# A graph layer and a mixture layer on one core: seven tiles instead of eight in the mixture's last block

## The chip, the cores and the metric

The kernel runs on one core of a Trainium2 chip. The metric is the device time of one execution in microseconds (us): lower is better. A core has five engines with queues of their own: TensorE (PE in the profile, its weight loads PEld), VectorE (DVE), ScalarE (ACT), GpSimd (POOL) and SyncE (SP), which here only issues DMAs. They are held together by semaphores alone.

## What is computed

There are 10000 tokens of 512 channels. A graph layer (edge messages, two matmuls with batch normalisation over all tokens) is followed by a mixture layer. The change touches the mixture layer alone; `x` below is the input plus the graph layer's output.

```python
grouped = x.reshape(B, S // t, t, D)                 # groups of t = 16 tokens
cont_logits = einsum('bgtd,des->bgtes', grouped, controller) + tie
cont_perm = (cont_logits == max over the 16 tokens)  # 16 experts x 4 sets
intermediate = einsum('bgtd,desf->bgtesf', grouped, f1)
inner = relu(einsum('bgtesf,bgtes->bgesf', intermediate, cont_perm))
inter2 = einsum('bgesf,esfd->bgesd', inner, f2)
result = einsum('bgesd,bgtes->bgtd', inter2, cont_perm)
out = x + result                                     # input: layernorm(x)
```

Each group of 16 tokens is computed apart from the others, so tokens can be cut into tiles at any multiple of 16.

## The kernel before, in words

The graph layer runs first: the edges, then the up and down matmuls. It leaves its second activation, transposed, in the DRAM tensor `h2T`. Then `mixture` (L834) starts. It takes the tokens in **tiles** of 128 (`P`) and the tiles in **blocks** of 8 (`TB`), so a block is 1024 tokens (`BW`) and there are 10 blocks (`NB`, 10000 / 1024 rounded up): 80 tiles. 10000 tokens are 78.125 tiles. The ninth block ends at token 9216, and the last one is put so that it ends at token 10000: `row` (L901) has it begin at 10000 - 1024 = 8976. Its first 240 tokens are therefore computed twice, with the same result.

A tile has a **front** half and a **back** half. The front of tile j does: bring in 256 columns of `h2T` for two tiles (`load_h`, L1033), apply silu (`nonlinear`, L1265), turn it (`turn_g`, L1310) and add it to x (`new_tile`, L1165), store that sum in `x1d` (`store_x1`, L1047), normalise it (`stats`, `norm`), turn it again (`turn_x`, L1323), multiply by the controller (`logits`, L1332), find the maxima (`select`, L1189), turn the choice (`spread` on PE, `turn_p`, L1342), and sum the chosen tokens into `yT` (`sums`, L1347, copied by ACT in `to_yT`, L1272). When all tiles of a block have been through that, four `inner` steps (L1417) multiply the block's whole `yT` by `f1`; their relu (L1010) is shared by DVE and ACT and fills `inner_bd`. The back of tile j then does: spread the choice over rows (`rows`, L1374, and `back_rows`, L1213), four `unit` steps of matmuls with `f2` (`inter`, L1386, L1401 is their line), whose results ACT copies (L1293) and DVE takes the remainder of (L1226), eight matmuls of `final` (L1413, L1414), an add of x (`result`, L1229), and the store (`store_out`, L1059); x comes back from `x1d` by `load_back` (L1052).

The order of all this is written out by hand in one generator, `schedule(front, back)` (L924), which every engine walks and from which it picks its own steps. `blocks` (L912) calls it 11 times, unrolled: the front of block k goes with the back of block k - 1. In step m of the eight steps of a call, the engines do `sums` of front tile m, `logits` and `turn_x` of front tile m + 1, `turn_g` of front tile m + 2, and the whole back of tile m. `inner` 0 of the front block is at the end of the call, `inner` 1 to 3 are in step 0 of the next one. The 11th call has no front (`k` is None): it is a tail of eight steps of back alone. No step of the mixture is inside a hardware loop, and every wait is on a constant.

TensorE's part of one step with front and back is, in order: `turn_p` (L1345), `rows` (L1382), 32 matmuls of L1401, `turn_g` (L1319), `turn_x` (L1329), `sums` (L1367), `logits` (L1339), `final` (L1413, L1414). All of them are 32-bit, and those of L1401, L1433 and L1339 show in the trace as two matmuls each.

Of the kernel before, what the change touches and what calls it, by code (L numbers as in the profile page):

```python
# [9 lines left out]
ACT = mybir.ActivationFunctionType  # L10
AX = mybir.AxisListType

N, H = 10000, 512
# [20 lines left out]
TB = 8  # L34
BW = TB * P
NB = -(-N // BW)
F2P = 4
QB = ES // GT
GH = GB // 2
# [794 lines left out]
def mixture(nc, sem, psum, ident, mhalf, x, h2T, x1d, vec, controller, f1, f2, out, stats2):  # L834
# [3 lines left out]
    with ExitStack() as ctx:  # L838
# [62 lines left out]
        def row(k, j):  # L901


            if isinstance(k, int) and k * TB + j >= (NB - 1) * TB:
                return N - BW + (k - (NB - 1)) * BW + j * P
            return k * BW + j * P

        def by2(t, par, of):

            return (t - par) * (of // 2) + of  # L910
# [8 lines left out]

        def exists(k, j):  # L920

            return k is not None and not (isinstance(k, int) and k == NB - 1 and j >= TB)

        def schedule(front, back):  # L924

            if front is not None and static(front, 1):
                yield "silu", (0, 0, KH)  # L930
                yield "silu", (1, 0, KH)
                yield "turn_g", 0
                yield "stats", 0
                yield "norm", 0
                yield "turn_x", 0
                yield "logits", 0
                yield "turn_g", 1
                yield "stats", 1
                yield "select", 0
                yield "norm", 1  # L940
            for m in range(TB):
                new, next_ = exists(front, m + 2), exists(front, m + 1)
                u = m * QB
                if front is not None:
                    yield "spread", m
                if back is not None:
                    yield "rows", m
                if back is not None and m == 0:
                    yield "inner", 1
                    yield "unit", u  # L950
                    yield "low", u
                    if new:
                        yield "turn_g", m + 2
                    yield "inner", 2
                    yield "unit", u + 1
                    yield "low", u + 1
                    if new:
                        yield "stats", m + 2
                    if next_:
                        yield "turn_x", m + 1  # L960
                    yield "inner", 3
                    yield "unit", u + 2
                    yield "low", u + 2
                    if next_:
                        yield "logits", m + 1
                    yield "unit", u + 3
                    yield "low", u + 3
                    if front is not None:
                        yield "sums", m
                elif back is not None:  # L970
                    yield "unit", u
                    yield "low", u
                    yield "unit", u + 1
                    yield "low", u + 1
                    yield "unit", u + 2
                    yield "low", u + 2
                    yield "unit", u + 3
                    if new:
                        yield "turn_g", m + 2
                    yield "low", u + 3  # L980
                    if new:
                        yield "stats", m + 2
                    if next_:
                        yield "turn_x", m + 1
                    if front is not None:
                        yield "sums", m
                    if next_:
                        yield "logits", m + 1
                else:
                    if new:  # L990
                        yield "turn_g", m + 2
                        yield "stats", m + 2
                    if next_:
                        yield "turn_x", m + 1
                    yield "sums", m
                    if next_:
                        yield "logits", m + 1
                if next_:
                    yield "select", m + 1
                if new:  # L1000
                    yield "norm", m + 2
                if exists(front, m + 3 + (m + 1) % 2):
                    yield "silu", ((m + 4) // 2, (m % 2) * KH // 2, (m % 2 + 1) * KH // 2)
                if back is not None:
                    yield "final", m
                    yield "result", m
            if front is not None:
                yield "inner", 0
# [13 lines left out]
        with nc.Block() as block:  # L1022
            @block.sync
            def _(sp):
# [8 lines left out]
                def load_h(k, p):  # L1033
                    pair = k * (TB // 2) + p
                    if not static(pair, 2):
                        sp.wait_ge(t1, (pair - 1) * 2)
                    sp.dma_start(h2[p % 2][:, :, :], h2T[:, :, bass.ds(row(k, 2 * p), 2 * P)].rearrange("m p n -> p m n"))\
                        .then_inc(ldh[p % 2], 16)

                def load_x(k, j):  # L1040
# [49 lines left out]

                blocks(sp, body)
                for b in range(2):
                    sp.wait_ge(ots[b], 16 * (TB // 2) * NB)

            @block.gpsimd
            def _(pool):
# [37 lines left out]
                def body(k, kb):  # L1134
                    for what, n in schedule(k, kb):
                        if what == "spread" and kb is None:
                            keep(k, n)
                        if what == "rows" and k is not None:
                            keep(k, n)
                        if what == "stats":  # L1140
                            root(k, n)
                        if what == "norm":
                            split(k, n)
# [118 lines left out]
            def _(act):  # L1262
                act.wait_ge(nrm[5], 1)

                def nonlinear(k, p, c0, c1):  # L1265
                    pair = k * (TB // 2) + p
                    act.wait_ge(ldh[p % 2], by2(pair, p % 2, 16))
                    for c in range(c0, c1):
                        nc.scalar.activation(h2[p % 2][:, c, :], h2[p % 2][:, c, :], ACT.Silu, bias=sh[:, c:c + 1],
                                             scale=sc[:, c:c + 1]).then_inc(gr, 1)  # L1270

                def to_yT(k, j, c, r):  # L1272
# [36 lines left out]
            def _(pe):  # L1309
# [76 lines left out]
                def inter(k, kb, u):  # L1386
                    j, b, q = u // QB, u % QB, unit_of(kb, u)
                    if b < 2:

                        pe.wait_ge(yr, (k * TB + j if k is not None else NB * TB) * KH)  # L1390
                    if static(kb, 1) and u == 0:
                        pe.wait_ge(wf2, 16 * F2P)
                    if j == 0:

                        pe.wait_ge(inv, (kb * QB + b + 1) * 2)
                        pe.wait_ge(ina, (kb * QB + b + 1) * 2)
                    if not static(q, QB):
                        pe.wait_ge(ilr, q - QB + 1)
                    for i in range(NS):
                        e = QE * b + i  # L1400
                        last = nc.tensor.matmul(bI[b][32 * i:32 * i + 32, :],  # L1401
                                                ibd[:, e, j, :, :].rearrange("p s g -> p (s g)"), f2s[:, e, :],
                                                start=True, stop=True)
                    last.then_inc(ip, 1)

                def final(k, kb, j):
                    pe.wait_ge(rr, kb * TB + j + 1)
                    if not static(kb * TB + j, 1):
                        pe.wait_ge(otr, kb * TB + j)
                    pe.wait_ge(yr, (k * TB + j) * KH + 2 if k is not None else NB * TB * KH)  # L1410
                    for b in range(QB):
                        pe.wait_ge(ilr, unit_of(kb, j * QB + b) + 1)
                        nc.tensor.matmul(bF[:, :], rbd[:, b, :], ihi[b][:, :], start=(b == 0), stop=False)  # L1413
                        nc.tensor.matmul(bF[:, :], rbd[:, b, :], ilo[b][:, :], start=False, stop=(b == QB - 1))\  # L1414
                            .then_inc(fp, 1)

                def inner(k, q):  # L1417

                    if q == 0:
                        if static(k, 1):  # L1420
                            pe.wait_ge(wf1, 16 * KH)
                        pe.wait_ge(yr, (k + 1) * TB * KH)
                    else:
                        if q == 1 and not static(k, 1):
                            pe.wait_ge(otr, k * TB)
                        if q >= 2:
                            pe.wait_ge(inv, (k * QB + q - 1) * 2)
                            pe.wait_ge(ina, (k * QB + q - 1) * 2)
# [107 lines left out]
```

## Time and profile before

| | us |
|---|---|
| three runs | 2109.22, 2110.25, 2110.86 |
| median | 2110.25 |
| the profiled execution, its own time | 2105.35 |
| its span | 2103.6 |
| mean granted clock of TensorE in it | 0.972 of full |
| the mixture's share of the span | about the last 890 us |

The profiled execution is one more run, 4.9 us below the median of the three. Its span goes from its first instruction to the last DMA; 1.75 us of its own time lie around the span. All steps and rows in this document are in us from the start of that span. In the trace's rows, a matmul's length is modelled and neighbours overlap: the distance from one start to the next says what an instruction takes of the engine. An idle time in brackets behind a row says how long the engine had nothing to do before it, and what ended that; "issue" is an idle time for which the profile shows no one that was waited for. A row of busy time by windows gives the stretch, its length, then busy time and (instructions) of PE, PEld, DVE, ACT and POOL, and last TensorE's granted clock, the share of the DMA engines' time and GB/s. A row of waits gives who waited for whom: us in total, times, the longest.

### The profile page before, as it was taken

What the parts mean: (1) busy time and instruction counts of PE and PEld (TensorE: products, weight loads), DVE (VectorE), ACT (ScalarE), POOL (GpSimd) and SP (SyncE); (2) the same over time, 40 slices, a digit from 0 to 9 for tenths busy, and PEclk for the clock granted to TensorE, in tenths of its full rate; (3) what the DMA queues carried; (4) which work ended last, traced back from release to release, by engine and by line L of the source; (5) the groups of instructions that cost most, each with busy time, mean ns of one, the idle gap of its engine ahead of it and who ended that gap; (6) DMA issues with size and microseconds to landing.
All of it is one profiled execution on the core that took longest, in us unless ns stands there. A gap on an engine that the chain in (4) does not pass through costs nothing. (4 is left out here: it accounts for less than half of the span.)

```text
span 2103.6 us, 42031 instructions
## 1 busy us (share of the span) xinstructions
PE 1892.0 (90%) x15720; PEld 1362.7 (65%) x15720; DVE 1194.2 (57%) x2533; ACT 1003.9 (48%) x1742; POOL 386.7 (18%) x481
## 2 busy tenths in 40 slices
PE   0777389999999979999999678999999999999999
PEld 0233178888888858888888565665666666656564
DVE  1457266666566443333333356776766767667666
ACT  0354123333333265565656255565655656556553
POOL 1577230000000000000000141222222222222210
PEclk9998699999999989999999889999999999999999
DMA  9887655666566353343433283343433434334322
GB/s 378 213 156 130 121 154 158 192 181 170 156 190 183 116 183 129 138 154 118 174 117 136 79 288 110 122 131 117 137 117 108 145 108 145 107 117 137 113 75 76
DMA packets 182816, 309.18 MB, mean 147 GB/s; under 512 B 33065, under 2 KB 107305, under 8 KB 179594
## 3 DMA queue, kind: packets, MB, share of 16 engines
q1 hardware_dynamic: 169674, 285.35, 43.5%
q0 software_dynamic: 8960, 20.98, 5.2%
q8 instruction: 101, 1.65, 0.3%
q10 hardware_dynamic: 4032, 0.80, 0.2%
q14 instruction: 49, 0.40, 0.1%
HBM read 172.20 MB, written 134.87 MB: 146 GB/s over the span
## 5 line engine op out<-in xcount | busy, mean ns | idle before, releaser
L1401 PE MATMUL bank<-f2s,inner_bd 128*32 128x512 f32 x2560 | 299.0, 596 | 1.9 <-DVE inner_bd L1012 1.4
L1293 ACT ACTIVATE inter_hi<-bank 128x512 fp32r<-128x512 f32 x320 | 191.1, 597 | 223.1 <-PE bank L1401 221.0
L1226 DVE TENSOR_TENSOR inter_lo<-bank,inter_hi 128x512 fp32r<-128x512 f32 x320 | 220.9, 690 | 100.3 <-ACT inter_hi L1293 98.8
L608 ACT ACTIVATE h1o<-bank,b_by_channel 128x500 f32<-128x500 f32 x160 | 108.5, 678 | 326.7 <-PE bank L423 326.7
L421 PE MATMUL bank<-ahi,w_hi 128*128 128x500 f32 x640 | 250.7, 392 | 14.6 <-DVE alo L762 14.6
L421 PE MATMUL bank<-hhi,w_hi 128*128 128x500 f32 x640 | 251.3, 393 | 2.5 <-DVE hlo L569 2.5
L423 PE MATMUL bank<-hhi,w_lo 128*128 128x500 f32 x640 | 249.6, 390 | 0.0
L422 PE MATMUL bank<-alo,w_hi 128*128 128x500 f32 x640 | 249.2, 389 | 0.0
L422 PE MATMUL bank<-hlo,w_hi 128*128 128x500 f32 x640 | 249.0, 389 | 0.0
L423 PE MATMUL bank<-ahi,w_lo 128*128 128x500 f32 x640 | 248.8, 389 | 0.0
L575 DVE BATCH_NORM_STATS2 stats<-h1o 128x500 f32 (+1 forms) x160 | 103.6, 676 | 162.4 <-ACT h1o L608 162.4
L762 DVE TENSOR_TENSOR alo<-a_whole,ahi 128x500 fp32r<-128x500 f32 x160 | 108.8, 680 | 106.2 <-ACT ahi L798 106.2
L1275 ACT ACTIVATE yT<-bank 128x512 f32<-128x512 f32 x320 | 165.4, 604 | 6.8 <-PE bank L1367 1.1
L1401 PEld LDWEIGHTS bank<-f2s,inner_bd 128*32 128x32 f32 x2560 | 73.7, 109 | 136.2 <-issue 127.5
L768 DVE BATCH_NORM_STATS2 stats<-h2o 128x500 f32 (+1 forms) x80 | 52.6, 678 | 175.6 <-ACT h2o L806 175.6
L421 PEld LDWEIGHTS bank<-ahi,w_hi 128*128 128x128 f32 x640 | 120.6, 188 | 42.3 <-DVE alo L762 18.0
L1413 PE MATMUL bank<-inter_hi,back_bd 128*128 128x512 f32 x320 | 132.6, 414 | 9.4 <-ACT yT L1275 8.6
L421 PEld LDWEIGHTS bank<-hhi,w_hi 128*128 128x128 f32 x640 | 120.6, 189 | 26.7 <-DVE hlo L569 2.9
L423 PEld LDWEIGHTS bank<-ahi,w_lo 128*128 128x128 f32 x640 | 120.7, 189 | 25.1
L422 PEld LDWEIGHTS bank<-hlo,w_hi 128*128 128x128 f32 x640 | 120.8, 189 | 24.7
L423 PEld LDWEIGHTS bank<-hhi,w_lo 128*128 128x128 f32 x640 | 120.6, 188 | 24.8
L422 PEld LDWEIGHTS bank<-alo,w_hi 128*128 128x128 f32 x640 | 120.9, 189 | 23.9
(124 smaller groups left out, 3182.6 us busy)
## 6 DMA issues: line engine op xcount, KB each, us to landing
h1T<-h1o SPq DMA_DIRECT2D x19, 2000.0 KB, 8.1
h1in<-h1T SPq DMA_DIRECT2D x19, 2000.0 KB, 9.6
aggregate<-zeros SPq DMA_DIRECT2D x20, 1024.0 KB, 8.2
h2in<-h2T SPq DMA_DIRECT2D x40, 512.0 KB, 4.1
x<-in_x SPq DMA_DIRECT2D x80, 256.0 KB, 2.8
x<-x SPq DMA_DIRECT2D x80, 256.0 KB, 3.6
x_back<-x SPq DMA_DIRECT2D x80, 256.0 KB, 3.2
out<-x_back SPq DMA_DIRECT2D x80, 256.0 KB, 2.8
```

What stands on the lines that cost most here:

```text
L421: nc.tensor.matmul(out, w_hi[:, k, cols], a_hi[:, k, :], start=(k == 0), stop=False)
L422: nc.tensor.matmul(out, w_hi[:, k, cols], a_lo[:, k, :], start=False, stop=False)
L423: last = nc.tensor.matmul(out, w_lo[:, k, cols], a_hi[:, k, :], start=False, stop=(k == chunks - 1))
L575: nc.vector.bn_stats(stats1[:, m, bass.ds(c * 6, 6)], h1o[b][:, m, :]).then_inc(str_, 1)
L608: nc.scalar.activation(h1o[b][:, m, :], mb[m % 4][:, 0:CW], ACT.Identity, bias=b1c[:, m:m + 1]).then_inc(evr, 1)
L762: nc.vector.tensor_tensor(alo[b][:, k, :], aw[:, k, :], ahi[b][:, k, :].bitcast(F32), ALU.subtract).then_inc(lor, 1)
L768: nc.vector.bn_stats(stats2[:, m, bass.ds(c * 6, 6)], h2o[b][:, m, :]).then_inc(str_, 1)
L1226: nc.vector.tensor_tensor(ilo[u % QB][:, :], bI[u % QB][:, :], ihi[u % QB][:, :].bitcast(F32), ALU.subtract).then_inc(ilr, 1)
L1275: nc.scalar.activation(yT[:, c:c + 2, :, j * GB + r * GH:j * GB + (r + 1) * GH], bY[c // 2][r][:, :].rearrange("p (c e g) -> p c e g", c=2 ...
L1293: nc.scalar.activation(ihi[n % QB][:, :], bI[n % QB][:, :], ACT.Copy).then_inc(ihr, 1)
L1401: last = nc.tensor.matmul(bI[b][32 * i:32 * i + 32, :], ibd[:, e, j, :, :].rearrange("p s g -> p (s g)"), f2s[:, e, :], start=True, stop=True)
L1413: nc.tensor.matmul(bF[:, :], rbd[:, b, :], ihi[b][:, :], start=(b == 0), stop=False)
```

## The change

The number of tiles becomes a constant of its own, `NT` = 79 (10000 / 128 rounded up), and the last block has `TL` = 7 tiles, from token 10000 - 896 = 9104 on. A new helper `tiles(k)` gives the number of tiles of a block, and `exists` asks for it. `schedule` runs over the larger of the two counts: in the call with the front of the last block and the back of the ninth, step 7 has a back but no front, and the 11th call has seven steps. The last pair of the last block is one tile wide: its load of `h2T` and its silu have 128 columns in place of 256. `inner` and its relu keep the width of eight tiles, and the eighth place of `yT` keeps what the ninth block left there; nothing reads the result. Waits that were worked out from eight tiles are worked out from `NT`.

```diff
+NT = -(-N // P)
+TL = NT - (NB - 1) * TB
...
-            if isinstance(k, int) and k * TB + j >= (NB - 1) * TB:
-                return N - BW + (k - (NB - 1)) * BW + j * P
+            if k * TB + j >= (NB - 1) * TB:
+                j += (k - (NB - 1)) * TB
+                return N - TL * P + j * P
...
-            return k is not None and not (isinstance(k, int) and k == NB - 1 and j >= TB)
+            return k is not None and k * TB + j < NT
+        def tiles(k):
+            return 0 if k is None else TL if k == NB - 1 else TB
...
-            for m in range(TB):
+            for m in range(max(tiles(front), tiles(back))):
+                ahead, behind = m < tiles(front), m < tiles(back)
-                if front is not None:
+                if ahead:
                     yield "spread", m
-                if back is not None:
+                if behind:
                     yield "rows", m
-                if back is not None and m == 0:
+                if behind and m == 0:
...
-                    if front is not None:
+                    if ahead:
                         yield "sums", m
-                elif back is not None:
+                elif behind:
...
-                if back is not None:
+                if behind:
                     yield "final", m
                     yield "result", m
...
+                    width = min(2, tiles(k) - 2 * p) * P if p < TB // 2 else 2 * P
-                    sp.dma_start(h2[p % 2][:, :, :], h2T[:, :, bass.ds(row(k, 2 * p), 2 * P)]...
+                    sp.dma_start(h2[p % 2][:, :, 0:width], h2T[:, :, bass.ds(row(k, 2 * p), width)]...
...
-                    sp.wait_ge(ots[b], 16 * (TB // 2) * NB)
+                    sp.wait_ge(ots[b], 16 * ((NT + 1 - b) // 2))
...
-                        if what == "rows" and k is not None:
+                        if what == "rows" and n < tiles(k):
                             keep(k, n)
...
-                        nc.scalar.activation(h2[p % 2][:, c, :], h2[p % 2][:, c, :], ACT.Silu, ...
+                        nc.scalar.activation(h2[p % 2][:, c, 0:width], h2[p % 2][:, c, 0:width], ACT.Silu, ...
...
-                        pe.wait_ge(yr, (k * TB + j if k is not None else NB * TB) * KH)
+                        pe.wait_ge(yr, (k * TB + j if k is not None else NT) * KH)
...
-                    pe.wait_ge(yr, (k * TB + j) * KH + 2 if k is not None else NB * TB * KH)
+                    pe.wait_ge(yr, min((k * TB + j) * KH + 2, NT * KH) if k is not None else NT * KH)
...
-                        pe.wait_ge(yr, (k + 1) * TB * KH)
+                        pe.wait_ge(yr, (k * TB + tiles(k)) * KH)
```

## Rows read from the trace of the kernel before

**Rows 1.** The page: busy time of each engine, share of the span, instructions.

```profile
PE 1892.0 (90%) x15720; PEld 1362.7 (65%) x15720; DVE 1194.2 (57%) x2533; ACT 1003.9 (48%) x1742; POOL 386.7 (18%) x481
```

**Rows 2.** Busy time by windows: steps 5, 6, 7, transition, tail.

```profile
2013.12:2022.36 9.24, 9.24 (x78) 5.89 (x77) 7.25 (x15) 5.05 (x9) 2.68 (x5) 1.00 0.26 85
2022.36:2031.14 8.78, 8.78 (x74) 5.45 (x73) 5.26 (x10) 5.01 (x9) 1.95 (x3) 1.00 0.21 63
2031.14:2039.42 8.28, 7.38 (x62) 3.90 (x60) 4.39 (x7) 4.46 (x8) 0.29 (x1) 1.00 0.22 65
2039.42:2057.25 17.83, 15.32 (x557) 10.77 (x557) 7.49 (x14) 5.39 (x12) 0.00 (x0) 1.00 0.10 32
2057.25:2100.39 43.14, 43.14 (x309) 19.99 (x307) 28.39 (x42) 16.73 (x28) 0.00 (x0) 1.00 0.27 86
```

**Rows 3.** Timeline of PE, from step 4's end in the tenth call to the end.

```profile
2012.88 0.40 PE L1414 MATMUL bank<-inter_lo,back_bd 128*128 128x512 f32 x1
...
2017.29 0.66 PE L1319 MATMUL bank<-ident,h2in 128*128 128x128 f32 x4
2017.79 0.60 PE L1329 MATMUL bank<-ident,xn 128*128 128x128 f32 x4
...
2020.43 0.47 PE L1413 MATMUL bank<-inter_hi,back_bd 128*128 128x512 f32 x1
...
2022.13 0.40 PE L1414 MATMUL bank<-inter_lo,back_bd 128*128 128x512 f32 x1
...
2030.91 0.40 PE L1414 MATMUL bank<-inter_lo,back_bd 128*128 128x512 f32 x1
...
2037.43 0.47 PE L1413 MATMUL bank<-inter_hi,back_bd 128*128 128x512 f32 x1 [0.90 <-ACT yT L1275]
...
2039.11 0.39 PE L1414 MATMUL bank<-inter_lo,back_bd 128*128 128x512 f32 x1
...
2093.86 0.39 PE L1414 MATMUL bank<-inter_lo,back_bd 128*128 128x512 f32 x1
...
2100.00 0.39 PE L1414 MATMUL bank<-inter_lo,back_bd 128*128 128x512 f32 x1
```

**Rows 4.** SP's and DVE's timelines: a load of x, its add, and the last add.

```profile
2083.16 2.08 SPq L1057 DMA_DIRECT2D x_back<-x  x1
```

```profile
2088.14 0.69 DVE L1233 TENSOR_TENSOR x_back<-bank,x_back 128x512 f32<-128x512 f32 x1 [0.82 <-PE bank L1414]
...
2100.43 0.69 DVE L1233 TENSOR_TENSOR x_back<-bank,x_back 128x512 f32<-128x512 f32 x1 [0.82 <-PE bank L1414]
```

**Rows 5.** DMA issues of the mixture: KB each, median us to landing.

```profile
x_back<-x SPq DMA_DIRECT2D x77, 256.0 KB, 3.2
...
h2in<-h2T SPq DMA_DIRECT2D x32, 512.0 KB, 4.1
```

**Rows 6.** SP's and ACT's timelines: last load of h2T, first silu on it.

```profile
1980.93 0.38 SPq L1037 DMA_DIRECT2D h2in<-h2T  x1
```

```profile
1993.30 1.11 ACT L1269 ACTIVATE h2in<-h2in,shift,scale 128x256 f32<-128x256 f32 x2
```

**Rows 7.** PE's waits in two transitions, 2039.4 to 2057.2 and 1955.9 to 1974.2.

```profile
PE bank L1433 <- issue: 2.0, 2, 1.2
PE bank L1401 <- issue: 0.4, 1, 0.4
```

```profile
PE bank L1433 <- issue: 2.8, 3, 1.6
```

**Rows 8.** Windows of 1200 to 1300; PE's timeline at the mixture's start.

```profile
1200.00:1300.00 100.00, 71.28 (x987) 53.02 (x987) 57.15 (x154) 50.59 (x98) 37.49 (x54) 0.85 0.60 205
```

```profile
1217.81 0.42 PE L1345 MATMUL bank<-eye,perm_new 128*128 128x64 f32 x1 [2.83 <-DVE perm_new L1202]
1218.04 1.11 PE L1319 MATMUL bank<-ident,h2in 128*128 128x128 f32 x4
1218.94 1.06 PE L1329 MATMUL bank<-ident,xn 128*128 128x128 f32 x4
```

More of the change, by code:

```diff
@@ L984, in schedule @@
                         yield "turn_x", m + 1
-                    if front is not None:
+                    if ahead:
                         yield "sums", m
@@ L1036, in load_h @@
                         sp.wait_ge(t1, (pair - 1) * 2)
-                    sp.dma_start(h2[p % 2][:, :, :], h2T[:, :, bass.ds(row(k, 2 * p), 2 * P)].rearrange("m p n -> p m n"))\
+                    width = min(2, tiles(k) - 2 * p) * P if p < TB // 2 else 2 * P
+                    sp.dma_start(h2[p % 2][:, :, 0:width], h2T[:, :, bass.ds(row(k, 2 * p), width)].rearrange("m p n -> p m n"))\
                         .then_inc(ldh[p % 2], 16)
@@ L1267, in nonlinear @@
                     act.wait_ge(ldh[p % 2], by2(pair, p % 2, 16))
+                    width = min(2, tiles(k) - 2 * p) * P if p < TB // 2 else 2 * P
                     for c in range(c0, c1):
-                        nc.scalar.activation(h2[p % 2][:, c, :], h2[p % 2][:, c, :], ACT.Silu, bias=sh[:, c:c + 1],
+                        nc.scalar.activation(h2[p % 2][:, c, 0:width], h2[p % 2][:, c, 0:width], ACT.Silu, bias=sh[:, c:c + 1],
                                              scale=sc[:, c:c + 1]).then_inc(gr, 1)
```

## The prediction

> **What bounds the kernel now.** I read the page first, for the share of each engine: PE is busy for 90% of the span and nobody else for more than 65% [rows 1]. An average over stages proves nothing about the last one, so the second view is the busy time by windows, cut at the step borders around the place that changes [rows 2]. The reader is to see three kinds of stretch. In steps 5 and 6 of the tenth call PE is busy for the whole window (9.24 of 9.24, 8.78 of 8.78) while DVE, the next one, has 7.25 and 5.26. In the tail, from the second of its eight steps on, it is again PE for 43.14 of 43.14, with DVE at 28.39. Between them lies the transition, the `inner` steps and the first back tile, 17.83 long with 15.32 busy. So PE sets the pace in all that a tile costs, and nothing waits ahead of it except 0.90 in step 7, for ACT's copy of `yT` [rows 3]. The third view is PE's own timeline, for the price of one step [rows 3]. The fourth, of SP, DVE and ACT, is for the covers [rows 4 to 6].
>
> **Part 1: the tail loses a step.** The 11th call has seven steps instead of eight. The last matmuls of two neighbouring `final` in the tail start at 2093.86 and 2100.00 [rows 3]: a step is 6.14. Seven such steps follow one another with the same work. PE is full in them, so all of it is on the path: **-6.14**. What lies behind the last matmul stays: the add from 2100.43 for 0.69, and then its store and the store's landing [rows 4].
>
> **Part 2: the tenth call loses the front of one tile.** Steps 0 to 4 issue what they issued before. The front of tile 7 was spread over three steps: `turn_g` in step 5, `turn_x` and `logits` in step 6, `turn_p` and `sums` in step 7. I don't add up matmuls, since the trace has whole steps of nearly every mix needed. From last `final` matmul to last `final` matmul, step 5 took 2022.13 - 2012.88 = 9.25, step 6 took 8.78 and step 7 took 8.20 [rows 3]. After the change step 5 lacks `turn_g`, as step 6 did before: 8.78. Step 6 lacks `turn_x` and `logits` as well, as step 7 did before: 8.20, with the 0.90 wait for `yT`, which moves here since no `logits` stands between `sums` and `final` any more. Step 7 is back alone, as a step of the tail: 6.14. Sum 23.12 against 26.23: **-3.11**. A check by starts: in step 5, `turn_g`, `turn_x`, `sums` and `logits` stand together from 2017.29 to the first `final` matmul at 2020.43, 3.14 [rows 3], and what remains of 9.25 is 6.11, against the 6.14 of the tail. So the two ways agree to 0.03.
>
> **Part 3: what stands at nothing, and its cover.** The last load of `h2T` halves, and so does its silu. Before, the load was issued at 1980.93 and its first silu ran at 1993.30 [rows 6], 12.4 later against 4.1 to land [rows 5]; the silu's 1.11 for two lies on ACT, which has 5.05 in a step of 9.24 [rows 2]. If that cover were gone it would cost at most 4.1 once. DVE, ACT and POOL lose tile 7's front too, beside PE. In step 7 `final` 7 now waits for all of `yT`, but tile 6's copies follow its `sums` one step earlier and end before the units of step 7 need the same banks. `load_back` of tile 7 has less time, as a step shrinks from 8.20 to 6.14; the tail shows that this is enough: the load issued at 2083.16 was the slowest to issue, 2.08, with 3.2 as the median to landing, and the add that needs it ran at 2088.14 and had waited for PE [rows 4, 5]. With the cover gone that is 2.08 + 3.2 - 4.98 = 0.3. No step that remains is moved past another on SP or POOL, and no wait is added that has a later releaser than the one it replaces. SP's wait for all stores at the head of the 11th call comes as before right after step 7.
>
> **Part 4: the transition.** Its instructions are the same; `inner` keeps its width. But there are pauses in it for which the profile shows nobody: 2.0 and 0.4 here, and 2.8 in the transition one block earlier [rows 7], while steps of the tail and steps 5 and 6 have none [rows 2]. All blocks have the same code there, so where a pause falls seems to depend on the position in the instruction stream, and the change takes about 33 matmuls and their weight loads out ahead of this transition. I take 0, because nothing says in which direction a pause would move. The bounds: all pauses gone, -2.4; the larger sum of 2.8, and one pause of 1.6 more in a step that had none, +2.0.
> The Trainium skill ("Runtime: NRT & Kernel Launch", Instruction fetch mechanics) says that instructions are fetched in blocks ahead of use and that crossing a block's border is mostly hidden. By that rule a shift of the code costs nothing and the sum stays at its middle value without these bounds. The pauses of rows 7 speak against "hidden" in a run of short matmuls, if they are fetches; the trace does not show that they are.
>
> **The sum.** -6.14 - 3.11 + 0 = -9.25, which is just one full step of 9.25, as it should be when one tile of 80 goes. The profiled execution would take 2105.35 - 9.25 = 2096.10. The median of the three runs is 4.9 above it, so the forecast is **2110.25 - 9.25 = 2101.0**, or 0.44%. The measurement of this kernel can tell about 0.2% (4.2 us) from no change.
>
> **The rivals.**
> *A, forecast: a full step goes* (2101.0, own range 2098.0 to 2103.9: the bounds of part 4 and 0.8 for the spread of the three runs). For it: PE full in every stretch that shrinks. 0.77.
> *B, the pauses move much*, beyond A's bounds or to them: 2098 or a little under. Against it: both transitions read have over 2 of them. 0.09.
> *C, only the tail's step is won* because the tenth call's last steps are held by another engine or a transfer once the front work is out of them: 2104.1. For it: the 0.90 wait for ACT shows that these steps can be held by others. Against it: DVE has 4.39 and ACT 4.46 in the 8.28 of step 7, and the tail's steps run at 6.14 with just that work [rows 2]. 0.08.
> *D, the change doesn't do what it says*, or the step comes back elsewhere: 2110.25. That would need an eighth step in the 11th call; `tiles(9)` is 79 - 72 = 7, and 79 tiles hold 10112 tokens, enough for 10000. 0.04.
> *E, slower: the clock.* The mechanism is that, from the changed step on, PE has less to do between waits and the chip grants it the lower of its two clocks, 1.2 instead of 2.4 GHz. At the mixture's start, after an idle time of 2.83, the four turns took 0.90 from start to start [rows 8] against 0.50 at the full clock of step 5 [rows 3], and the stretch with 71% busy had a mean grant of 0.85 [rows 8]. About 52 us of PE work lie behind step 7 (15.32 + 43.14 - 6.14) and would take twice that: 2101.0 + 52 = 2153. It turns the sign once more than 9.25 us of PE's work run at half clock, and shows as slower by over 0.2% from 13.5 on. Against it: the transition, with its pauses up to 1.2, and the tail ran with a grant of 1.00 throughout [rows 2, 7], and no idle time longer than those is added. 0.02.
> The Trainium skill ("TensorE: Matmul & The Clock Gate", HAM oscillation) describes such a fall to half clock where PE waits for data between short groups of matmuls. The trace agrees at the mixture's start, and in the stretch that changes it shows no such wait.
>
> **How the numbers follow.** The time is A's. The low end takes in A's lower bound, 2097.8; the high end reaches past A's 2103.9 to C's 2104.1 with some of the spread: 2104.6. D, E and a part of B are left out. Faster by over 0.2%: A, B, C, less their edges: 0.94. Within 0.2%: D, 0.04. Slower: E, 0.02.
>
> **What the changed profile would show.** PE with 15720 matmuls less 33 and less 44 (4 + 32 + 8 of a back tile), about 15643 with records lost. Steps 5, 6 and 7 of the tenth call at 8.8, 8.2 and 6.1, the 0.9 wait for `yT` ahead of `final` 6 and none ahead of `final` 7, seven steps of 6.14 at the end but for the first, and a clock of 1.00 there. Everything up to 2013 us as before. The forecast is wrong if step 7 is clearly longer than 6.14 (then C, and the wait names who), if the transition differs from 17.8 by over 2 (then B), if the clock falls (then E), or if time moves ahead of 2013 us, where nothing was changed and which I don't expect at all.

## The result, and the profile after

| | before | after |
|---|---|---|
| median of nine runs, us | 2109.22 (2105.81 to 2115.38) | 2094.86 (2092.02 to 2103.09) |
| ratio, 95% interval | | 0.9939 (0.9923 to 0.9956) |
| the profiled execution, its own time | 2105.35 | 2101.61 |
| its span | 2103.6 | 2099.8 |

The kernel is faster, by 12.9 us as the ratio has it (9.3 to 16.2). The forecast was 9.25, with a median of 2101.0 and a low end of 2097.8: the direction is right, the median lies 2.9 below the low end. The three executions made first took 2101.61, 2103.09 and 2099.11, the six later ones 2092.02 to 2095.82; of the kernel before, the three made first took 2109.22 to 2110.86 and the six later ones 2105.81 to 2115.38.

The profiled pair is only 3.74 apart, less than the forecast. The first thing to find out is where the two traces part. The page's first part, after, to be read beside [rows 1]:

```profile
PE 1885.8 (90%) x15643; PEld 1359.4 (65%) x15643; DVE 1185.6 (56%) x2518; ACT 999.0 (48%) x1733; POOL 384.2 (18%) x477
```

77 matmuls and 77 weight loads are gone. The timeline of PE after, the last `final` matmuls of the tenth call's steps 4 to 7 and of the last two steps (the line that was L1414 is L1424, and L1413 is L1423), against [rows 3]:

```profile
2018.95 0.40 PE L1424 MATMUL bank<-inter_lo,back_bd 128*128 128x512 f32 x1
...
2027.75 0.39 PE L1424 MATMUL bank<-inter_lo,back_bd 128*128 128x512 f32 x1
...
2034.27 0.47 PE L1423 MATMUL bank<-inter_hi,back_bd 128*128 128x512 f32 x1 [0.90 <-ACT yT L1285]
...
2035.94 0.39 PE L1424 MATMUL bank<-inter_lo,back_bd 128*128 128x512 f32 x1
...
2042.08 0.39 PE L1424 MATMUL bank<-inter_lo,back_bd 128*128 128x512 f32 x1
...
2090.08 0.39 PE L1424 MATMUL bank<-inter_lo,back_bd 128*128 128x512 f32 x1
...
2096.22 0.39 PE L1424 MATMUL bank<-inter_lo,back_bd 128*128 128x512 f32 x1
```

From last matmul to last matmul, step 5 takes 8.80, step 6 takes 8.19 and step 7 takes 6.14; the tail's step takes 6.14. The wait of 0.90 for ACT has moved from `final` 7 to `final` 6. Busy time by windows after, transition and tail, against [rows 2]:

```profile
2042.38:2059.62 17.24, 14.50 (x558) 10.54 (x557) 7.49 (x14) 5.40 (x12) 0.00 (x0) 1.00 0.11 34
2059.62:2096.61 36.99, 36.99 (x265) 17.10 (x263) 24.32 (x36) 14.35 (x24) 0.00 (x0) 1.00 0.26 86
```

So the place that was changed did what was worked out for it. But the last matmul of step 4 stands at 2018.95, and it stood at 2012.88 before: 6.07 were lost ahead of the change, in code that is the same. To find them I took, from DVE's timeline, the distances between neighbouring results. Steps inside a call are 9.24 in both kernels, within 0.1. What differs is the distance from a call's last result to the next call's first one, over the transition:

| transition | 1 | 2 | 3 | 4 | 5 | 6 | 7 | 8 | last |
|---|---|---|---|---|---|---|---|---|---|
| before | 21.53 | 21.59 | 20.69 | 21.14 | 20.95 | 22.14 | 21.67 | 22.18 | 17.92 |
| after | 22.07 | 21.59 | 21.83 | 21.95 | 22.05 | 23.15 | 22.22 | 22.57 | 17.32 |

The first eight are 5.54 more in all after, and the first result of all came 0.57 later. Transition 1 shows one part of it. Timeline of PE, before and then after, from `inner` 0 of block 1 on (L1433 is L1443 after):

```profile
1351.46 1.99 PE L1433 MATMUL bank<-yT,f1s 128*32 128x64 f32 x128
1353.39 0.30 PE L1345 MATMUL bank<-eye,perm_new 128*128 128x64 f32 x1
1353.52 0.64 PE L1382 MATMUL bank<-perm_T,rep 128*128 128x128 f32 x4
1354.09 1.75 PE L1433 MATMUL bank<-yT,f1s 128*32 128x64 f32 x106
1356.80 0.52 PE L1433 MATMUL bank<-yT,f1s 128*32 128x64 f32 x20 [0.95 <-issue]
```

```profile
1352.06 1.99 PE L1443 MATMUL bank<-yT,f1s 128*32 128x64 f32 x128
1353.99 0.30 PE L1355 MATMUL bank<-eye,perm_new 128*128 128x64 f32 x1
1354.12 0.64 PE L1392 MATMUL bank<-perm_T,rep 128*128 128x128 f32 x4
1354.69 1.75 PE L1443 MATMUL bank<-yT,f1s 128*32 128x64 f32 x106
1358.22 0.52 PE L1443 MATMUL bank<-yT,f1s 128*32 128x64 f32 x20 [1.78 <-issue]
```

In both, PE stops behind 128 + 1 + 4 + 106 = 239 matmuls of the transition, with no one named that it waited for, once for 0.95 and once for 1.78. These are the pauses of part 4 of the prediction. Below, a pause's place is the number of matmuls since `inner` 0 began. Transition 1 has them at 239, 365 and 491 in both kernels, and in all nine transitions ahead of the change (the one behind the first block's `inner` 0 counted as well) those that the two traces both show stand at the same places. From one transition to the next they move forward by 14 to 16. What differs is how long they are.

The pauses are not all of the 5.54. Windows of the kernel after, in transitions 6 and 8:

```profile
1800.53:1803.95 3.42, 3.42 (x16) 1.53 (x15) 0.69 (x1) 0.49 (x1) 0.00 (x0) 0.50 0.02 5
1967.79:1971.20 3.41, 3.41 (x100) 3.08 (x104) 1.28 (x2) 0.60 (x1) 0.00 (x0) 0.50 0.20 74
```

The granted clock is 0.50 there, 1.2 GHz in place of 2.4. The profile before has no such stretch between 1290 and the last matmul, and in the profile after a single window from 1290 to 2095 still rounds to 1.00. PE had been idle just ahead of them, for 1.91 until 1799.29 and for 2.11 until 1966.46; the pause of 2.33 that ended at 1617.62 was not followed by one. If all idle times of PE over 0.15 are taken off, the first eight transitions take 18.2 to 18.4 in both profiles, but for these two with 20.07 and 19.50. So of the 5.54, 2.5 are idle time of PE, and 3.0 are the rest, nearly all of it in the two transitions with the half clock.

**The theories.** P: the pauses come at fixed places in PE's stream of instructions and last differently in each execution; the change is worth its 9.25, and the rest of the 12.9 is chance. Q: the changed build has shorter pauses of its own, and 12.9 would come again. Two more came up on the way: R, a pause belongs to a place in the schedule, not in the stream, and T, the last transition became shorter because pauses moved in it.

### The profile page after: what moved, and what is told of

Its sections match the earlier page's. It is cut to its first block and busy times, and to the rows that moved or that the text cites. A ratio compares the mean times of both kernels' runs of the same rounds, so it can differ in the third digit from the quotient of the medians.

```text
span 2099.8 us, 41816 instructions
## 1 busy us (share of the span) xinstructions
PE 1885.8 (90%) x15643; PEld 1359.4 (65%) x15643; DVE 1185.6 (56%) x2518; ACT 999.0 (48%) x1733; POOL 384.2 (18%) x477
## 3 DMA queue, kind: packets, MB, share of 16 engines
q8 instruction: 101, 1.65, 0.3%
## 5 line engine op out<-in xcount | busy, mean ns | idle before, releaser
L1423 PE MATMUL bank<-inter_hi,back_bd 128*128 128x512 f32 x316 | 131.2, 415 | 9.4 <-ACT yT L1285 8.6
L423 PEld LDWEIGHTS bank<-hhi,w_hi 128*128 128x128 f32 x640 | 120.7, 189 | 26.7 <-DVE hlo L571 2.9
```

The costliest lines, as they stand in the source:

```text
L423: nc.tensor.matmul(out, w_hi[:, k, cols], a_hi[:, k, :], start=(k == 0), stop=False)
```

## The experiments

**Both kernels again, and each part of the change alone.** The first two are the two kernels as they are. The tail alone is the kernel before with this edit:

```diff
-            for m in range(TB):
+            for m in range(TB if front is not None else TB - 1):
...
-                    sp.wait_ge(ots[b], 16 * (TB // 2) * NB)
+                    sp.wait_ge(ots[b], 16 * ((TB * NB - b) // 2))
```

The front alone is the changed kernel with these:

```diff
-                return N - TL * P + j * P
+                return N - BW + j * P
...
+        def backs(k):
+            return 0 if k is None else TB
...
-            for m in range(max(tiles(front), tiles(back))):
-                ahead, behind = m < tiles(front), m < tiles(back)
+            for m in range(max(tiles(front), backs(back))):
+                ahead, behind = m < tiles(front), m < backs(back)
...
+                    s = t if t < NT else t - 2
-                    sp.wait_ge(x1s[j % 2], by2(t, j % 2, 16))
+                    sp.wait_ge(x1s[j % 2], by2(s, j % 2, 16))
...
-                    sp.dma_start(x1b[j % 2][:, :], x1d[bass.ds(t * P, P), :]).then_inc(ldb[j % 2], 16)
+                    sp.dma_start(x1b[j % 2][:, :], x1d[bass.ds(s * P, P), :]).then_inc(ldb[j % 2], 16)
...
-                    sp.wait_ge(ots[b], 16 * ((NT + 1 - b) // 2))
+                    sp.wait_ge(ots[b], 16 * (TB // 2) * NB)
...
-                    pe.wait_ge(pTr, kb * TB + j + 1)
+                    pe.wait_ge(pTr, min(kb * TB + j + 1, NT))
```

The tail alone leaves out the last 128 rows of the output, and the front alone gets them wrong. Both are here for their time.

> The kernel before, unchanged, run beside itself. Theory P (TensorE's unexplained pauses in the inner steps come every 256 instructions of its stream and last differently in each run): the ratio to before is 1.000, single runs spread by up to 10 us, and a new profile has the steps at 9.24 and 6.14 as before and differs from the first one only in how long the pauses of the nine transitions are, by up to 5 us in all. Rival Q (a kernel has its own pauses, set by where its code lies): the pauses of this profile are within 1 us in all of the first one's 24.4.

> The changed kernel again. Theory P: 9.25 us less than before in the long run, ratio 0.9956, and within 2 us of it here. Rival Q: the extra gain belongs to the changed build and comes again, 12 to 15 us less, ratio 0.993 to 0.994, with pauses shorter in all by 3 to 6 us than in the profile of before taken here.

> The front of all 80 tiles, but the back of 79: the last 128 rows of the output are left out. The steps: 6.14 us less than before, the tenth call's last steps at 9.25, 8.8 and 8.2 and seven steps in the 11th call. Theory P: ratio 0.9971, within 2 us. Rival Q: a time that the removed step doesn't explain, off by 3 us or more.

> The front of 79 tiles with the old placement, the back of 80; the 80th back works on what the eighth place held before and on x of another tile, so the last 128 rows are not the reference's. The steps: 3.1 us less than before, the tenth call's last steps at 8.8, 8.2 and 6.14, eight steps in the 11th call. Theory P: ratio 0.9985, within 2 us. Rival Q: off by 3 us or more.

| | ratio to before, 95% interval | us less, as forecast | us less, measured |
|---|---|---|---|
| before again | 0.9998 (0.9988 to 1.0009) | 0 | 0.4 |
| after again | 0.9958 (0.9942 to 0.9973) | 9.25 | 8.9 |
| tail alone | 0.9974 (0.9963 to 0.9984) | 6.14 | 5.5 |
| front alone | 0.9987 (0.9976 to 0.9997) | 3.11 | 2.7 |

(Measured: one minus the ratio, times the 2108.7 of before in these rounds.) The two halves add up to the whole, 5.5 + 2.7 = 8.2 against 8.9. The steps in the traces are as expected: in the front alone, steps 5 to 7 take 8.77, 8.19 and 6.14 between results; in the tail alone 9.22, 8.78 and 8.24. The 12.9 did not come again.

The runs of before in these rounds went from 2103.01 to 2113.52, over 10 us with one and the same program. Its second profile shows where that is. The first eight transitions take 174.55 in place of 171.89, and the first result is 0.57 later; that is 3.23 together, and the two own times, 2108.26 and 2105.35, are 2.91 apart. The pauses stand where they stood. One is longer and another shorter (the one at 223 in transition 2 has 0.58 in place of 1.28), but PE's idle times in the eight transitions come to 25.4 in place of 25.5. The 2.66 go with the clock: this profile has two stretches at 0.50, from 1616.34 and from 1964.49, next to pauses of 1.60 and 1.78, where the first had none. So P's "differs only in how long the pauses are" failed. In the changed kernel the profile here has 173.43 for the eight where the first had 177.43, and its first result 1.99 earlier: 5.99 in all, and the own times are 5.97 apart. It has no stretch at half clock there; of the 4.00, 0.9 are idle time and 3.1 the rest. So the spread between executions, as far as these profiles go, is in the transitions, in their pauses and in falls of the clock, and in what comes ahead of the mixture's first result.

P's fixed places hold. Of Q, the pauses of all ten transitions are within 1 us for the kernel before (24.8 and 24.4) and not for the changed one (24.3 and 26.7). They are not 3 to 6 us shorter in the changed kernel than in the kernel before (24.3 against 24.8 here), and the gain did not come again. Q is out.

**The changed kernel a third time, its stream shifted, more DMA traffic, and narrower matmuls.** Four edits of the changed kernel (the first one none):

```diff
+                for i in range(64):
+                    nc.tensor.transpose(bA[:, (i % KH) * P:(i % KH + 1) * P], ident[:, :], ident[:, :])
                 blocks(pe, body)
```

```diff
+        scratch = nc.dram_tensor("scratch_f1", [NB, P, ES * FF], F32, kind="Internal").ap()
+        sxt = sem("scratch_loaded")
...
+                        if what == "inner" and n == 0:
+                            sp.dma_start(scratch[k], f1[0:P].rearrange("p e s f -> p (e s f)")).then_inc(sxt, 16)
...
+                sp.wait_ge(sxt, 16 * NB)
```

```diff
-                                    bD[q % 2][32 * s:32 * s + 32, (e % QE) * 64:(e % QE) * 64 + 64],
-                                    f1s[:, c, es * FF:(es + 1) * FF], yT[:, c, es, :],
+                                    bD[q % 2][32 * s:32 * s + 32, (e % QE) * 64:(e % QE) * 64 + tiles(k) * GB],
+                                    f1s[:, c, es * FF:(es + 1) * FF], yT[:, c, es, 0:tiles(k) * GB],
```

> The changed kernel once more, to see which of its two ratios so far (0.9939 and 0.9958) comes again. Theory P (the change is worth its 9.25 us of matmul steps, the rest is the chance of the pauses): 0.9956, and within 0.001 of it. Rival Q (the changed build has shorter pauses of its own): 0.994 or less.

> The changed kernel with 64 turns of the identity ahead of the mixture, in about 10 us in which TensorE has nothing to do; they put 128 instructions into its stream and add no time of their own. Theory P: the pauses of a transition keep their distance of about 126 matmuls, but all lie 64 matmuls earlier (block 1: 175, 301 and 427 matmuls behind its inner 0 in place of 239, 365 and 491), and the time is that of the changed kernel within 2 us. Rival R (a pause belongs to a place in the schedule, a wait that the profile doesn't name): they stay at 239, 365 and 491.

> The changed kernel with one more transfer of 1 MB from DRAM to DRAM in each transition, issued behind the store of the last result, read by nobody. Theory P with fetches over the same DMA engines: the pauses stay where they are, the first ones of a transition get longer, by 1 to 3 us in each of the ten, and the kernel takes 10 to 30 us longer than the changed one. Rival R: the pauses are as before and so is the time, within 2 us, since no load or store of x is on the path.

> The changed kernel with 56 columns in place of 64 in the inner matmuls of the last block, whose eighth place nobody reads. If the stream of instructions sets the pace of these short matmuls: 128 of them take 1.99 us as with 64 columns, and the time is that of the changed kernel. Rival S (the columns set it): 56/64 of 1.99 us, 1.74 us, four times, 1.0 us less.

| | ratio to before, 95% interval |
|---|---|
| after, third time | 0.9949 (0.9935 to 0.9963) |
| shifted by 64 turns | 0.9951 (0.9938 to 0.9965) |
| 1 MB more in each transition | 1.0032 (1.0019 to 1.0046) |
| inner of 56 columns in the last block | 0.9953 (0.9939 to 0.9968) |

*The shift.* Timeline of PE of the shifted kernel, transition 1, to be held against the two above:

```profile
1351.08 1.99 PE L1443 MATMUL bank<-yT,f1s 128*32 128x64 f32 x128
1353.01 0.30 PE L1355 MATMUL bank<-eye,perm_new 128*128 128x64 f32 x1
1353.14 0.64 PE L1392 MATMUL bank<-perm_T,rep 128*128 128x128 f32 x4
1353.71 0.86 PE L1443 MATMUL bank<-yT,f1s 128*32 128x64 f32 x42
1355.94 0.77 PE L1443 MATMUL bank<-yT,f1s 128*32 128x64 f32 x40 [1.38 <-issue]
```

128 + 1 + 4 + 42 is 175, where it was 239: 64 earlier, exactly the turns put in. The three pauses of the transition stand at 175, 301 and 427. R is out: a pause belongs to a place in the instruction stream. The distance between two neighbours is 126 to 128 matmuls; each has a weight load of its own, so that is 252 to 256 instructions and a few waits. The page counts the fetches of instructions as a DMA queue of its own, in the kernel before with 101 packets and 1.65 MB, 16 KB each:

```profile
q8 instruction: 101, 1.65, 0.3%
```

The Trainium skill ("Runtime: NRT & Kernel Launch", Instruction fetch mechanics) gives the block of a fetch as 16 KiB or 256 instructions: the trace agrees, in size and in distance. What the Trainium skill says in the same section, that crossing a border is mostly hidden, holds in the ordinary steps, where no pause shows, and not in a run of short matmuls, of which PE takes one in 15.5 ns (128 in 1.99). The trace has a start and a length for each of these packets, and they tie the pauses to the fetches. In the thirteen profiles of this document PE goes on, behind 364 such pauses of the mixture, 1.4 after a packet of this queue has landed (the median; 1.2 to 1.6 in nine of ten). So it does behind the idle time of 1.36 or more at place 541 of transition 6, which the view puts down to DVE. Next to one another in a transition the packets start 3.2 to 5 apart, and in no profile under 3.2, while the 128 short matmuls that one brings are 1.99 of work. That is why PE runs dry there.

The 64 turns themselves took 10.12 and the first turn behind them began at 1208.68, against 1204.04 in the kernel without them; by the mixture's first result, 1286.51 against 1286.43, that was caught up.

*More traffic.* The kernel takes 0.8% more than the changed one, some 17 us. The pauses stand at the same places, 258 in transition 8, and some are far longer. Timeline of PE there:

```profile
1972.29 1.99 PE L1448 MATMUL bank<-yT,f1s 128*32 128x64 f32 x128
1974.22 0.30 PE L1360 MATMUL bank<-eye,perm_new 128*128 128x64 f32 x1
1974.35 0.64 PE L1397 MATMUL bank<-perm_T,rep 128*128 128x128 f32 x4
1974.92 1.98 PE L1448 MATMUL bank<-yT,f1s 128*32 128x64 f32 x125
1983.68 0.43 PE L1448 MATMUL bank<-yT,f1s 128*32 128x64 f32 x3 [6.78 <-issue]
```

6.78, where the other profiles of the changed kernel have 1.70 to 2.11 (and 1.58 to 1.85 before). The first eight transitions take 191.07, against 173.4 to 177.4 in the three profiles of the changed kernel as it is. Nobody reads what is copied, and the steps between stay at 9.24, so no load or store of x was in the way. The fetches of instructions share the DMA engines with the data and wait behind it: here a packet of the copy, 64 KB, took from 1977.45 to 1981.31, the fetch that PE stood for began at 1981.31 and landed at 1982.26, and PE went on at 1983.68. Three more fetches of this profile begin within 0.01 of the end of such a packet. The pauses of all ten transitions come to 42.6, against 24.3 to 26.9 in the profiles of the changed kernel as it is, and PE had half its clock in three stretches, the longest from 1981.54 to 1988.37. That each of the ten gets longer, as P had it, isn't so: transition 2 is at 21.57 as before.

*Fewer columns.* The groups of L1443 in the last transition, first the kernel as it is, then with 56 columns (busy, mean ns, then the idle time before them):

```profile
L1443 PE MATMUL bank<-yT,f1s 128*32 128x64 f32 x512 | 8.8, 220 | 2.7 <-issue 2.7
```

```profile
L1443 PE MATMUL bank<-yT,f1s 128*32 128x56 f32 x512 | 7.9, 214 | 3.4 <-issue 3.4
```

The matmuls do get shorter, 128 of them from 1.99 to 1.78, so S is right about what sets their own length. But the pauses grow by 0.7 where the matmuls shrink by 0.9, and the transition takes 17.38 against 17.36. What paces the `inner` steps as a whole is the arrival of their instructions, 3.2 and more from fetch to fetch; faster matmuls come to the next border sooner and wait there. From the end of the pause at 171 to the end of that at 424 PE took 7.91 here, and 6.85 to 7.39 in the four profiles of the changed kernel as it is. Both of the expectation's lines of thought missed that. It is one profile with 56 columns, and the pauses vary by themselves, so that the narrower matmuls win nothing is likely and not shown.

**The last transition by itself.** It takes 17.32, 17.29, 17.36, 17.38 and (front alone) 17.31, where the matmuls taken out ahead have moved the pauses, and 17.92, 18.11 and (tail alone) 18.85 where they stand as before. Two more kernels change places: 35 small turns bring the changed kernel's pauses to where before has them, 92 bring those of before to where the changed kernel has them.

```diff
+                for i in range(35):      # 92 in the kernel before
+                    nc.tensor.transpose(bA[0:32, 0:32], ident[0:32, 0:32], ident[0:32, 0:32])
                 blocks(pe, body)
```

> The changed kernel with 35 small turns (32 x 32) of the identity ahead of the mixture. They shift its borders of 256 instructions so that those of the last transition lie where the kernel before has them (263, 391, 517 matmuls behind inner 0 in place of 171, 298, 424). Theory T (the last transition is 0.7 us shorter in the changed kernel, 17.3 against 18.0, because of where the borders fall): 18.0 between the two last results that enclose it, borders at 263, 391 and 517, and some 0.7 us more time than the changed kernel, which the timing can hardly tell. Rival U (it is shorter because less is queued on the other engines): 17.3 as before the shift.

> The kernel before with 92 small turns of the identity ahead of the mixture, which put its last transition's borders where the changed kernel has them (171, 298, 424). Theory T: 17.3 us for that transition in place of 17.9 to 18.1, and the time of before within 2 us plus what the turns take. Rival U: 18.0.

> The changed kernel a fourth time, for the mean of the ratio. Theory P with T: 9.25 + 0.7 = 9.95 us less, ratio 0.9953, within 0.001 of it. Rival Q: 0.994 or less.

| | ratio, 95% interval | last transition | all eight before it |
|---|---|---|---|
| after, 35 turns | 0.9944 (0.9926 to 0.9961) | 19.17 | 178.98 |
| before, 92 turns | 0.9996 (0.9985 to 1.0006) | 17.21 | 175.60 |
| after, fourth time | 0.9953 (0.9935 to 0.9971) | 17.54 | 176.39 |

Timeline of PE, last transition, the changed kernel with 35 turns:

```profile
2048.23 0.63 PE L1411 MATMUL bank<-f2s,inner_bd 128*32 128x512 f32 x3 [0.67 <-issue]
...
2052.35 0.31 PE L1443 MATMUL bank<-yT,f1s 128*32 128x64 f32 x5 [1.39 <-issue]
```

And the kernel before with 92:

```profile
2045.30 1.44 PE L1433 MATMUL bank<-yT,f1s 128*32 128x64 f32 x88 [0.65 <-issue]
...
2049.14 1.58 PE L1433 MATMUL bank<-yT,f1s 128*32 128x64 f32 x97 [1.10 <-issue]
...
2052.70 1.70 PE L1433 MATMUL bank<-yT,f1s 128*32 128x64 f32 x106 [0.81 <-issue]
```

The first has them at 263 and 391 (and 517), the second at 172, 299 and 425. The short transition went with the places and not with the kernel: T holds in its direction, U is out. With the pauses at 263, 391 and 517 it took 17.92, 18.11, 18.85 and 19.17, 18.5 on the mean; with 171, 298 and 424 (or one more each) and no added traffic 17.21 to 17.54, 17.3 on the mean. That is 1.2 and not the 0.7 that I expected, but a rough 1.2: the four of the first kind spread over 1.25, and the two profiles of the kernel before as it is give 0.7. At 235, 362 and 488, with 64 turns, it took 18.49. The ratios (0.9944 and 0.9996) show nothing of it: 1.2 is 0.0006 of the kernel, and the turns also move the pauses of the other nine transitions.

## Why the prediction was wrong, by its own steps

**Parts 1 and 2, the steps: right.** -6.14 and -3.11 were worked out; the trace after has 8.80, 8.19 and 6.14 for steps 5 to 7 against 8.78, 8.20 and 6.14 forecast, and six distances of 6.14 in the tail. Each part alone gave its share: 5.5 and 2.7, with intervals of 3.4 to 7.8 and 0.6 to 5.1.

**Part 3, the covers: right.** Step 7 alone with its load of x runs at 6.14, and the one-tile load and silu of the last pair show no wait. The 0.90 moved to step 6 as forecast.

**Part 4, the transition at 0: the first step that failed.** "I take 0" should have been about -1.2, by the mean of four profiles against seven (-0.7 if of the four only the two of the kernel before as it is count). The mechanism was there, that a shift of the stream moves the pauses, and -1.2 lies in its bounds of -2.4 and +2.0, but I said that nothing tells in which direction. Something did: the trace gives the place of every pause, and the number of matmuls taken out gives the new one. The pause at 263 moved to 298, 35 matmuls later, for 33 taken out with their weight loads and waits. What I couldn't have read there is what the new places cost.

**The range: the second step that failed.** "0.8 for the spread of the three runs" took three runs made together for the spread of the kernel. Single executions of before went from 2103.01 to 2115.43 in all rounds, and in profiles of one kernel the first eight transitions alone took 173.4 to 177.4, by their pauses and by falls of the clock, neither of which the range allowed for ahead of the change. The hint stood in the numbers: the profiled execution lay 4.9 below the median, six times what I allowed. [rows 7] also showed that the pauses of one transition are not those of the next. A median of nine from such runs can lie two or three us off. Had I allowed 3 for that, the range would have reached to 2095.6 and still missed by 0.7, and only with part 4 at -1.2 would it have held. A slip besides: A's "own range 2098.0 to 2103.9" is 2097.8 to 2103.8 by its own bounds and 0.8.

**What the change is worth.** The four ratios of the unpadded changed kernel are 0.9939, 0.9958, 0.9949 and 0.9953; their mean, 0.9950, is 10.6 us. The steps' 9.25 and the last transition's 0.7 to 1.2 are 10.0 to 10.4, which the intervals do not tell from 10.6. The medians of the three later rounds, 2099.62, 2098.56 and 2099.68, lie in the range. The first session's ratio was off this by 0.0011, inside its interval, and no cause but chance was found for it; why its six later executions were so fast stays open, for these have no profiles. So how far the median fell below the range is in part luck of the executions, as far as is known.

**The rivals.** B, the pauses move much, was the nearest, and had 0.09; it is true in kind (-1.2) but not in the size it named. C and D gave way to the steps, and E to a granted clock of 1.00 in the last transition and the tail. But what E describes does happen ahead of the change, in both kernels: between 1290 and the last matmul the first profile after and the second one before have two stretches at half clock each, the first one before none. Transitions with one take 1.1 to 1.8 more than PE's idle times explain. With 0.02, and for the changed stretch alone, the prediction had no term for it.

**Two sentences of the prediction to correct.** That the ordinary steps have no pauses is right, and the likely reason is that the borders are there too, but PE takes 17 matmuls in 2 us and not 128: 128 of them are 15 us, and the fetches there start 10 to 18 apart. And "I don't expect at all" that time moves ahead of 2013: it did, by 6.07 in the profile, by longer pauses and two falls of the clock, both of which vary between executions of one program.

## What to carry to other kernels

Where an engine is full from start to end and the trace has a whole step of every mix that the change makes, differences of such steps foretell the new ones, here to a few hundredths of a us, and no matmul has to be added up. Before giving a range, ask what differs between executions of one and the same program, and allow for that by the spread of all of them, the profiled one too. Look at the clock in windows of a few us, since one of hundreds rounds a short fall away. A stretch of very short matmuls can have a cost that belongs to no instruction: count its pauses' places from one transition to the next, and when code ahead of it goes or comes, work out where they fall.

## What the runs showed of the hardware that was not expected

- PE's pauses for no one named stand at fixed places of its instruction stream, 126 to 128 matmuls (with as many weight loads) apart, and last 0.2 to 2.4 from the second transition on, without added traffic (the very first pause, at 125, up to 4.7); 64 turns put in far ahead moved them by 64. They end 1.4 us after a 16 KB packet of the instruction queue has landed, and such packets never start less than 3.2 us apart.
- They grow with DMA traffic: up to 6.78 with 1 MB more in each transition, some 17 us on the kernel, with no load or store that the kernel needs on the path. Four fetches began within 0.01 us of the end of a 64 KB packet of the copy.
- Where they fall decides about a microsecond (0.7 to 1.2) in one transition of 17 to 19.
- The granted clock fell to half in single transitions, next to idle times of PE from 1.55 to 2.4, in some executions and not in others of the same kernel; such a transition is 1.1 to 1.8 longer.
- Matmuls that were 11% shorter in such a stretch (1.78 for 1.99) left the transition's length at 17.4, in one profile.
